# A fused decoder layer: the mixer's log decay spread by ScalarE in 16 copies, and the gate's projection, tanh and gating put ahead of the turning of y

## The chip, the cores and the metric

The kernel runs on one core of one Trainium2 chip. The metric is the device time of one execution in microseconds (us). Engines: PE (TensorE; PEld is its weight load), DVE (VectorE), ACT (ScalarE), POOL (GpSimd), SP (SyncE, which here issues DMAs only).

## The reference

One decoder layer over 32 sequences of 256 tokens of width 256: a mixer with a layer norm behind it, an attention over a context of 77 tokens, and a layer of 8 experts with 2 chosen per token. The change lies in the mixer alone:

```
zxBCdt = x @ in_proj_w.T                      # z, xc, Bm (8), Cm (64), dtm (64)
dt = softplus(Bm + dt_bias)
xh = silu(depthwise_causal_conv(xc, conv_w, conv_b)).reshape(B, L, 8, 64)
a_bar = exp(dt * -exp(A_log))
h = a_t[:, :, None, None] * h + b_t[:, None, None, :] * x_t[..., None]   # for every token t
y_t = einsum('bhdn,bn->bhd', h, c_t)
y = (y + xh * D_param) * silu(z)
x = layernorm(x + rms_norm(y, norm_w) @ out_proj_w.T)
```

## The kernel before, in words

The program is a chain of phases: mixer (`mixer_phase`), keys and values, attention, experts, finish. The mixer takes one sequence a turn. The recurrence is not run token by token. Within each half of 128 tokens (index c, `NT` = 2) it is a product with a weight matrix exp(sum of log decays) for each of the 8 heads. For that the log decay `l_dt` (128 tokens x 8 heads) is multiplied with the triangle `upto` into `lm` (128 x 8 x 128) for each half: this is **spread_l** (L732 to L739), one GpSimd product of 1024 columns a half. PE multiplies `lm` by the matrix `after` (**decay(c)**, L365 to L379), ACT takes the exponential (**exp_decay(c)**, L502 to L508), DVE weighs it with the scores (**weigh(c)**, L610 to L618), and PE forms y with it (**mix**, L393 to L405).

The work is a software pipeline written by hand. Each engine has a list of stages, each with a lag: in turn s the stage works on sequence s minus its lag. `run_steps` (L78 to L98) walks the list in order, with the first 4 and the last turns written out and the others in a loop of 2 sequences a round. There are 32 sequences and lags up to 2 on PE and ACT, so 34 steps there. An engine does its stages strictly in the order of its list, and waits on semaphores within each stage.

The order on PE (L435 to L437): in_x (the projection of xc), turn_y (y of two turns ago is turned into PSUM), in_z (the gate's projection), in_bc, step_size, scores, decay(0), turn_x, decay(1), out (the output projection), mix, mix_off.

The order on ACT (L533 to L535): take_xc, squares, y_high, tanh_z, take_bc, exp_decay(0), exp_rc, take_x, exp_decay(1), tanh_conv, softplus. The tables for tanh and exp and for ln alternate, so there are two table loads a turn, at tanh_z (L477) and at softplus (L531).

The order on DVE (L701 to L704): the high part of the next x, the first taps of the convolution, y_low, gate, bias_dt, mask_g, taps, weigh(0), weigh(1), taps, normalise, add_d, silu_conv, log_decay, residual.

The order on POOL (L787 to L788): x_low, inv_rms, scale_x, join (three products and sums that make y; L743 to L756), spread_l, inv_std. SP loads x two turns ahead and stores the result.

Two PSUM tiles bind stages together. `p23` holds the turned y (`ps_yT`) and also the two banks that decay(c) writes. y is split from it into a high part (y_high on ACT, L479 to L483) and a low part (y_low on DVE, L583 to L585), so decay(0) waits until y_low of the sequence before is done:

```
def y_low(b):
    dve.wait_ge(s_yhi, b.count(1, 1))
    dve.tensor_tensor(yT_lo[:, :, :], ps_yT, yT_hi[:, :, :].bitcast(F32), ALU.subtract).then_inc(s_ylo, 1)
```

`p45` holds the gate's projection, which tanh_z (L473 to L477) and gate (L575 to L581) read, and then the turned x.

Of the kernel before, what the change touches and what calls it, by code (L numbers as in the profile page):

```python
# [8 lines left out]
ALU = mybir.AluOpType  # L9
ACT = mybir.ActivationFunctionType  # L10
# [5 lines left out]
P = 128  # L16
# [3 lines left out]
NT = L // P  # L20
# [96 lines left out]
def mixer_phase(nc, n_seq, signals, following, xT, x, x1, w_in, w_out, norm_w, conv_w, conv_b, A_log, D_param, dt_bias, masks):  # L117
# [7 lines left out]
    H, N_STATE, D_CONV, DI = 8, 64, 4, 512  # L125
# [6 lines left out]
    with ExitStack() as ctx:  # L132
# [20 lines left out]
        upto, after, ident = mk[:, 0, :], mk[:, 1, :], mk[:, 2, :]  # L153
        spare = sb("spare", [P, 1])
# [21 lines left out]
        l_dt = sb("l_dt", [P, 2, NT * H])  # L176
        lm = sb("lm", [P, NT, H, P])
# [111 lines left out]
        def _(pe):  # L289
# [75 lines left out]
            def decay(c):  # L365
                def run(b):

                    if c == 0:
                        pe.wait_ge(s_lm, b.count(1, 1))
                        if not b.before(1):  # L370
                            pe.wait_ge(s_ylo, b.ago(1).count(1, 1))
                    else:
                        pe.wait_ge(s_exp, b.count(NT, 1))
                    for j in range(2):
                        last = pe.matmul(p23[:, j, :], after,
                                         lm[:, c, 4 * j:4 * j + 4, :].rearrange("p h t -> p (h t)"),
                                         start=True, stop=True)
                    last.then_inc(s_E, 1)
                return run  # L379
# [41 lines left out]
            def out(b):  # L421
# [11 lines left out]
                last.then_inc(s_out, 1)  # L433

            run_steps(pe, n_seq, [  # L435
                (in_x, 0), (turn_y, 2), (in_z, 0), (in_bc, 0), (step_size, 0), (scores, 1), (decay(0), 1), (turn_x, 1),
                (decay(1), 1), (out, 2), (mix, 1), (mix_off, 1)])  # L437

        @block.scalar
        def _(act):  # L440
            act.wait_ge(s_w_in, 16)
            for part in W_PARTS:
                act.activation(w_hi[:, :, part], w_stage[:, :, part], ACT.Copy).then_inc(s_whi_a, 1)
            act.wait_ge(s_load, 16 * N_LOADS)
            act.activation(a_neg[:, :], a_neg[:, :], ACT.Exp).then_inc(s_whi_a, 1)

            def take_xc(b):

                act.wait_ge(s_xc, b.count(1, 1))
                if b.before(1):  # L450
                    act.wait_ge(s_pow, 2)
                else:
                    act.wait_ge(s_conv, b.ago(1).count(12, 12))
                    act.wait_ge(s_sx, b.ago(1).count(1, 1))
                act.activation(xc_pad[:, :, D_CONV - 1:], ps_xc, ACT.Copy).then_inc(s_pad, 1)
                for m in range(MI):
                    last = act.activation(conv[:, m, :], ps_xc[:, m, :], ACT.Identity,  # L457
                                          bias=cb[:, m:m + 1], scale=cw[:, m, D_CONV - 1:D_CONV])
                last.then_inc(s_tap, 1)

            def squares(b):
                for c in range(NT):
                    act.wait_ge(s_y, b.count(NT, c + 1))
                    if c:
                        act.wait_ge(s_sq, b.count(NT, c))
                    elif not b.before(1):
                        act.wait_ge(s_sq, b.ago(1).count(NT, NT))
                    if not b.before(2) and c == 0:
                        act.wait_ge(s_ri, b.ago(2).count(2, 1))
                    act.activation(sq[:, :], y[:, b.par, c, :], ACT.Square, accum_out=ss[:, b.par, c:c + 1]  # L470
                                   ).then_inc(s_sq, 1)

            def tanh_z(b):  # L473
                act.wait_ge(s_z, b.count(1, 1))
                if not b.before(1):
                    act.wait_ge(s_zs, b.ago(1).count(1, 1))
                act.activation(z_t[:, :, :], p45[:, :, :], ACT.Tanh, scale=0.5).then_inc(s_zt, 1)  # L477

            def y_high(b):  # L479
                act.wait_ge(s_yT, b.count(1, 1))  # L480
                if not b.before(1):
                    act.wait_ge(s_out, b.ago(1).count(1, 1))
                act.activation(yT_hi[:, :, :], ps_yT, ACT.Copy).then_inc(s_yhi, 1)  # L483

            def take_bc(b):
                act.wait_ge(s_bc, b.count(1, 1))
                if not b.before(2):
                    act.wait_ge(s_g, b.ago(2).count(1, 1))
                for w in range(2):
                    last = act.activation(bc[:, b.par, w, :], ps_bc[N_STATE * w:N_STATE * w + N_STATE, :], ACT.Copy)  # L490
                last.then_inc(s_bcc, 1)

            def exp_rc(b):

                act.wait_ge(s_g, b.count(1, 1))
                act.wait_ge(s_gm, b.count(1, 1))
                if not b.before(1):
                    act.wait_ge(s_or, b.ago(1).count(1, 1))
                    act.wait_ge(s_cx, b.ago(1).count(1, 1))
                act.activation(rc[:, :], ps_rc, ACT.Exp).then_inc(s_rc, 1)  # L500

            def exp_decay(c):  # L502
                def run(b):
                    act.wait_ge(s_E, b.count(NT, c + 1))
                    if not b.before(1):
                        act.wait_ge(s_mt, b.ago(1).count(NT, c + 1))
                    act.activation(e_x[:, c, :, :].rearrange("p h t -> p (h t)"),
                                   p23[:, :, :].rearrange("p b t -> p (b t)"), ACT.Exp).then_inc(s_exp, 1)  # L508
                return run

            def take_x(b):
                act.wait_ge(s_T, b.count(1, 1))
                if not b.before(1):
                    act.wait_ge(s_Y, b.ago(1).count(NT, NT))
                    act.wait_ge(s_xd, b.ago(1).count(1, 1))
                    act.wait_ge(s_cx, b.ago(1).count(1, 1))
                act.activation(x_t[:, :, :], p45[:, :, :], ACT.Copy).then_inc(s_xt, 1)

            def tanh_conv(b):
                act.wait_ge(s_conv, b.count(12, 12))  # L520
                if not b.before(1):
                    act.wait_ge(s_sx, b.ago(1).count(1, 1))
                act.activation(conv_t[:, :, :], conv[:, :, :], ACT.Tanh, scale=0.5).then_inc(s_ct, 1)

            def softplus(b):
                act.wait_ge(s_na, b.count(1, 1))
                act.activation(v_ex[:, :], v_na[:, :], ACT.Exp).then_inc(s_dex, 1)
                act.wait_ge(s_dex, b.count(1, 1))
                if not b.before(1):
                    act.wait_ge(s_sp, b.ago(1).count(1, 1))  # L530
                act.activation(v_ln[:, :], v_ex[:, :], ACT.Ln, bias=1.0).then_inc(s_dln, 1)  # L531

            run_steps(act, n_seq, [  # L533
                (take_xc, 0), (squares, 2), (y_high, 2), (tanh_z, 0), (take_bc, 0), (exp_decay(0), 1), (exp_rc, 1),
                (take_x, 1), (exp_decay(1), 1), (tanh_conv, 0), (softplus, 0)])  # L535

        @block.vector
        def _(dve):
# [90 lines left out]
            def log_decay(b):  # L629
# [3 lines left out]
                                         op0=ALU.max, op1=ALU.add).then_inc(s_sp, 1)  # L633
                dve.wait_ge(s_sp, b.count(1, 1))
                if not b.before(2):
                    dve.wait_ge(s_lm, b.ago(2).count(1, 1))
                    dve.wait_ge(s_g, b.ago(2).count(1, 1))
                dve.tensor_tensor(l_dt[:, b.par, :].rearrange("p (c h) -> p c h", c=NT),
                                  v_sp[:, :].rearrange("p (c h) -> p c h", c=NT),
# [54 lines left out]
            def prep_once(b):  # L694
# [4 lines left out]
                    prep_out()  # L699

            run_steps(dve, n_seq, [  # L701
                (prep_once, 0), (x_high_next, 0), (taps(0, 1), 0), (y_low, 2), (gate, 0), (bias_dt, 0), (mask_g, 1),
                (taps(1, 2), 0), (weigh(0), 1), (weigh(1), 1), (taps(2, 3), 0), (normalise, 3), (add_d, 1),
                (silu_conv, 0), (log_decay, 0), (residual, 2)], spare=2)  # L704

# [1 line left out]
        def _(pool):  # L707
# [7 lines left out]
            def scale_x(b):  # L715
# [12 lines left out]
                                              x_t[:, c, :].rearrange("p (h d) -> p h d", h=H),  # L728
                                              d_b[:, :].unsqueeze(2).to_broadcast([P, H, HD]), ALU.mult)
                last.then_inc(s_xd, 1)  # L730

            def spread_l(b):  # L732

                pool.wait_ge(s_l, b.count(1, 1))
                if not b.before(1):
                    pool.wait_ge(s_E, b.ago(1).count(NT, NT))
                for c in range(NT):
                    last = pool.tensor_tensor(lm[:, c, :, :],
                                              l_dt[:, b.par, H * c:H * c + H].unsqueeze(2).to_broadcast([P, H, P]),  # L739
                                              upto.unsqueeze(1).to_broadcast([P, H, P]), ALU.mult)  # L740
                last.then_inc(s_lm, 1)

            def join(b):  # L743

# [38 lines left out]
            def x_low_next(b):  # L783
                if not (b.known() and b.value() + 1 >= n_seq):
                    x_low(b.ago(-1))

            run_steps(pool, n_seq, [  # L787
                (x_low_next, 0), (inv_rms, 2), (scale_x, 1), (join, 1), (spread_l, 0), (inv_std, 2)], spare=2)  # L788


class Unit:
# [1520 lines left out]
```

## Time and profile before

| | |
|---|---|
| median of 3 runs | 2477.99 us (2472.6 to 2484.72) |
| profiled execution | 2475.47 us, span in the profile 2473.7 us |
| busy over the whole span | PE 2201.1 us (89%), DVE 1793.5 (73%), ACT 1394.5 (56%), POOL 1243.3 (50%) |
| mean granted clock of PE | 0.944 |
| PE granted clock in 40 slices of the span | 9999999999997987999999999999988999999955 |
| DVE busy in the same slices, in tenths | 7888888888895312676776776776755777777778 |
| POOL busy in the same slices, in tenths | 3767677677664432032232232232244777766656 |

One slice is 62 us. The mixer fills the first 13 slices, some 790 us. The attention fills about slices 17 to 30. A busy share says how long an engine worked in a stretch, and not who waited for it; for that the views of waits and of the order in time are read.

### The profile page before, as it was taken

What the parts mean: (1) busy time and instruction counts of PE and PEld (TensorE: products, weight loads), DVE (VectorE), ACT (ScalarE), POOL (GpSimd) and SP (SyncE); (2) the same over time, 40 slices, a digit from 0 to 9 for tenths busy, and PEclk for the clock granted to TensorE, in tenths of its full rate; (3) what the DMA queues carried; (4) which work ended last, traced back from release to release, by engine and by line L of the source; (5) the groups of instructions that cost most, each with busy time, mean ns of one, the idle gap of its engine ahead of it and who ended that gap; (6) DMA issues with size and microseconds to landing.
All of it is one profiled execution on the core that took longest, in us unless ns stands there. A gap on an engine that the chain in (4) does not pass through costs nothing. (4 is left out here: it accounts for less than half of the span.)

```text
span 2473.7 us, 53288 instructions
## 1 busy us (share of the span) xinstructions
PE 2201.1 (89%) x15804; PEld 1917.0 (77%) x15805; DVE 1793.5 (73%) x4428; ACT 1394.5 (56%) x3046; POOL 1243.3 (50%) x1347
## 2 busy tenths in 40 slices
PE   7999999999995866999999999999968999999766
PEld 5777777777774755888888888888858999999733
DVE  7888888888895312676776776776755777777778
ACT  5556556565562321666666666666635666655433
POOL 3767677677664432032232232232244777766656
PEclk9999999999997987999999999999988999999955
DMA  4101111101001797233222212211136777776588
GB/s 143 31 26 38 34 30 38 34 30 38 30 29 51 259 327 237 82 107 110 63 63 64 64 62 63 66 61 62 59 113 221 233 254 237 246 233 221 164 282 269
DMA packets 169263, 295.27 MB, mean 119 GB/s; under 512 B 26204, under 2 KB 107620, under 8 KB 169188
## 3 DMA queue, kind: packets, MB, share of 16 engines
q1 hardware_dynamic: 155140, 257.62, 32.2%
q0 software_dynamic: 12960, 35.67, 4.0%
q10 hardware_dynamic: 1088, 1.07, 0.1%
q8 instruction: 37, 0.61, 0.1%
q14 instruction: 38, 0.31, 0.0%
HBM read 192.52 MB, written 101.77 MB: 119 GB/s over the span
## 5 line engine op out<-in xcount | busy, mean ns | idle before, releaser
L1460 ACT ACTIVATE b_wk_f<-b_ps_s,b_nmx 128x77 f32<-128x77 f32 x1024 | 233.7, 347 | 15.5 <-DVE b_nmx L1508 15.5
L570 DVE SCALAR_TENSOR_TENSOR a_conv<-a_xc_pad,a_cw,a_conv 128x256 f32<-128x256 f32 x384 | 236.6, 675 | 7.8 <-ACT a_conv L457 7.8
L1468 ACT ACTIVATE b_pT<-b_ps_pT 77x1024 f32<-77x1024 f32 x128 | 130.7, 1021 | 142.5 <-PE b_ps_pT L1366 142.5
L2056 POOL DMA_INDIRECT made_scratch<-c_o_s,c_to x142 | 151.0, 1064 | 90.9 <-issue 43.3
L112 PE MATMUL c_ps_h<-c_xT_hi,c_w 128*128 128x256 f32 x568 | 167.6, 295 | 26.0 <-DMA c_b_c<-in_c_b 18.7
L1524 DVE TENSOR_TENSOR b_oT_lo<-b_ps_oT,b_oT_hi 128x512 fp32r<-128x512 f32 x128 | 88.0, 688 | 134.9 <-ACT b_oT_hi L1474 133.2
L1928 ACT ACTIVATE c_hid<-c_ps_h,c_b_c 128x256 f32<-128x256 f32 x284 | 111.1, 474 | 104.9 <-issue 66.5
L112 PE MATMUL c_ps_o<-w,c_h_hi 128*128 x568 | 160.4, 282 | 6.6 <-DVE c_h_lo L1972 6.6
L1451 ACT ACTIVATE b_qT<-b_ps_q,b_bq_s 128x256 f32<-128x256 f32 x256 | 107.5, 472 | 100.3 <-PE b_ps_q L114 96.9
L113 PE MATMUL c_ps_h<-c_xT_lo,c_w 128*128 128x256 f32 x568 | 161.7, 285 | 0.0
L114 PE MATMUL c_ps_h<-c_xT_hi,c_w 128*128 128x256 f32 x568 | 161.5, 284 | 0.0
L1354 PE MATMUL b_ps_s<-b_kz,b_qT 128*128 128x154 f32 x1024 | 156.6, 295 | 4.9 <-ACT b_wk_f L1460 4.8
L114 PE MATMUL c_ps_o<-w,c_h_lo 128*128 x568 | 159.9, 282 | 0.0
L113 PE MATMUL c_ps_o<-w,c_h_hi 128*128 x568 | 159.8, 281 | 0.0
L112 PE MATMUL b_ps_q<-b_xT_hi,b_wq_hi 128*128 128x256 f32 x512 | 156.0, 305 | 2.4 <-DVE b_xT_lo L1500 1.5
L1972 DVE TENSOR_TENSOR c_h_lo<-c_hid,c_h_hi 128x1024 fp32r<-128x1024 f32 x71 | 94.8, 1335 | 86.3 <-ACT c_h_hi L1937 69.3
L112 PE MATMUL b_ps_out<-b_wo_hi,b_oT_hi 128*128 128x256 f32 x512 | 156.9, 306 | 0.0
L1718 POOL TENSOR_TENSOR b_e<-b_euler,b_gap 128x2 f32<-128x2 f32 x32 | 23.6, 736 | 256.6 <-DVE b_gap L1573 256.6
L1745 POOL DMA_INDIRECT sent_scratch<-b_x_t,b_pos x128 | 127.1, 993 | 46.3 <-issue 46.3
L114 PE MATMUL b_ps_q<-b_xT_hi,b_wq_lo 128*128 128x256 f32 x512 | 145.8, 285 | 0.0
L1354 PEld LDWEIGHTS b_ps_s<-b_kz,b_qT 128*128 128x128 f32 x1024 | 141.3, 190 | 5.6 <-issue 5.6
L113 PE MATMUL b_ps_q<-b_xT_lo,b_wq_hi 128*128 128x256 f32 x512 | 145.5, 284 | 0.0
(269 smaller groups left out, 7855.6 us busy)
## 6 DMA issues: line engine op xcount, KB each, us to landing
c_w<-parts_scratch SPq DMA_DIRECT2D x71, 1024.0 KB
c_xa<-sent_scratch SPq DMA_DIRECT2D x71, 260.0 KB
parts_scratch<-w SPq DMA_DIRECT2D x32, 512.0 KB, 3.3
d_got<-made_scratch SPq DMA_DIRECT2D x32, 512.0 KB, 5.2
keys_scratch<-k_k_s SPq DMA_DIRECT2D x8, 1232.0 KB, 6.1
b_kz<-keys_scratch SPq DMA_DIRECT2D x64, 154.0 KB, 2.8
b_vv<-values_scratch SPq DMA_DIRECT2D x32, 308.0 KB
a_xT_f<-in_xT SPq DMA_DIRECT2D x32, 256.0 KB, 3.0
```

The source lines that it names most:

```text
L112: eng.matmul(out, lh, rh, start=start, stop=False)
L113: eng.matmul(out, lh, rl, start=False, stop=False)
L114: return eng.matmul(out, ll, rh, start=False, stop=stop)
L570: dve.scalar_tensor_tensor(out=conv[:, m, :], in0=xc_pad[:, m, k:k + L], scalar=cw[:, m, k:k + 1], in1=conv[:, m, :], op0=ALU.mult, op1=AL ...
L1354: last = pe.matmul(s_scores[:, i, 2 * j:2 * j + 2, :], qT[:, u.par, i, P * j:P * j + P], kz[:, b.par, :, GM * g + i, :], start=True, stop= ...
L1451: last = act.activation(qT[:, u.par, i, :], ps_q[:, L * i:L * i + L], ACT.Identity, bias=bq_s[:, m:m + 1], scale=HD ** -0.5)
L1460: last = act.activation(pe_[:, u.par, c, :], s_scores[:, c // (C // GM), c % (C // GM), :], ACT.Exp, bias=nmx[:, u.par, c:c + 1])
L1468: act.activation(pT[:, u.par, :, :], ps_pT[0:LK, :, :], ACT.Copy).then_inc(s_pTc, 1)
L1745: pool.indirect_dma_start(routing.sent, bass.IndirectOffsetOnAxis(pos[:, b.par, 2 * c + n:2 * c + n + 1], 0), x2_t[:, b.par, c, :], None). ...
L1928: last = act.activation(hid[:, T * m:T * m + T], ps_h[t.par][:, m // 2, T * (m % 2):T * (m % 2) + T], ACT.Gelu, bias=b1_c[:, t.par, m:m + 1])
L1972: dve.tensor_tensor(h_lo[:, t.par, :], hid[:, :], h_hi[:, t.par, :].bitcast(F32), ALU.subtract).then_inc(s_hlo, 1)
L2056: pool.indirect_dma_start(routing.made, bass.IndirectOffsetOnAxis(to[:, t.slot, c:c + 1], 0), o_s[:, t.par, c, :], None).then_inc(s_sent[t ...
```

## The change

ScalarE takes over spread_l: for each half c it writes 8 copies of the triangle `upto`, each scaled by the log decay of one head (a scale per partition). There is one stage for each half, spread_l(0) after squares and spread_l(1) after y_high. PE's decay(c) waits for its half alone. On PE in_z comes ahead of turn_y; on ACT tanh_z comes ahead of y_high; on DVE gate comes ahead of y_low. GpSimd's list loses spread_l. log_decay, which writes `l_dt` again two sequences later, now waits for both halves.

```diff
@@ decay(c), on PE
+                    pe.wait_ge(s_lm, b.count(NT, c + 1))
                     if c == 0:
-                        pe.wait_ge(s_lm, b.count(1, 1))
                         if not b.before(1):
                             pe.wait_ge(s_ylo, b.ago(1).count(1, 1))
@@ PE's order
-                (in_x, 0), (turn_y, 2), (in_z, 0), (in_bc, 0), (step_size, 0), (scores, 1), (decay(0), 1), (turn_x, 1),
+                (in_x, 0), (in_z, 0), (turn_y, 2), (in_bc, 0), (step_size, 0), (scores, 1), (decay(0), 1), (turn_x, 1),
@@ ScalarE
+            def spread_l(c):
+                def run(b):
+
+                    act.wait_ge(s_l, b.count(1, 1))
+                    if not b.before(1):
+                        act.wait_ge(s_E, b.ago(1).count(NT, c + 1))
+                    for h in range(H):
+                        last = act.activation(lm[:, c, h, :], upto, ACT.Copy, scale=l_dt[:, b.par, H * c + h:H * c + h + 1])
+                    last.then_inc(s_lm, 1)
+                return run
@@ ScalarE's order
-                (take_xc, 0), (squares, 2), (y_high, 2), (tanh_z, 0), (take_bc, 0), (exp_decay(0), 1), (exp_rc, 1),
+                (take_xc, 0), (squares, 2), (spread_l(0), 1), (tanh_z, 0), (y_high, 2), (spread_l(1), 1), (take_bc, 0), (exp_decay(0), 1), (exp_rc, 1),
@@ log_decay, on DVE
-                    dve.wait_ge(s_lm, b.ago(2).count(1, 1))
+                    dve.wait_ge(s_lm, b.ago(2).count(NT, NT))
@@ DVE's order
-                (prep_once, 0), (x_high_next, 0), (taps(0, 1), 0), (y_low, 2), (gate, 0), (bias_dt, 0), (mask_g, 1),
+                (prep_once, 0), (x_high_next, 0), (taps(0, 1), 0), (gate, 0), (y_low, 2), (bias_dt, 0), (mask_g, 1),
@@ GpSimd
-            def spread_l(b):
-
-                pool.wait_ge(s_l, b.count(1, 1))
-                if not b.before(1):
-                    pool.wait_ge(s_E, b.ago(1).count(NT, NT))
-                for c in range(NT):
-                    last = pool.tensor_tensor(lm[:, c, :, :],
-                                              l_dt[:, b.par, H * c:H * c + H].unsqueeze(2).to_broadcast([P, H, P]),
-                                              upto.unsqueeze(1).to_broadcast([P, H, P]), ALU.mult)
-                last.then_inc(s_lm, 1)
@@ GpSimd's order
-                (x_low_next, 0), (inv_rms, 2), (scale_x, 1), (join, 1), (spread_l, 0), (inv_std, 2)], spare=2)
+                (x_low_next, 0), (inv_rms, 2), (scale_x, 1), (join, 1), (inv_std, 2)], spare=2)
```

## Rows read from the trace of the kernel before

**Rows 1.** Stretches: us, busy time of each engine, granted clock, DMA share, GB/s.
```profile
core 0: us, PE busy (x) PEld busy (x) DVE busy (x) ACT busy (x) POOL busy (x), PEclk, DMA share, GB/s
201.20:601.20 400.00, 369.03 (x2384) 306.91 (x2384) 354.76 (x615) 234.99 (x377) 276.55 (x222) 1.00 0.11 33
```

**Rows 2.** Waits from 200 to 600 us: us in total, times, longest.
```profile
PE a_p L418 <- POOL a_y L756: 26.6, 17, 1.6
...
PE a_p L375 <- ACT a_e_x L507: 4.4, 18, 0.2
```

**Rows 3.** Order in time, ACT, one turn: start, duration, instruction, idle before.
```profile
401.20 1.03 ACT L455 ACTIVATE a_xc_pad<-a_p 128x1024 f32<-128x1024 f32 x1 [2.72 <-PE a_p L114]
402.12 1.93 ACT L457 ACTIVATE a_conv<-a_p,a_cb,a_cw 128x256 f32<-128x256 f32 x4
403.91 0.65 ACT L470 ACTIVATE a_sq<-a_y 128x512 f32<-128x512 f32 x1
...
405.38 1.01 ACT L483 ACTIVATE a_yT_hi<-a_p 128x1024 fp32r<-128x1024 f32 x1
406.40 1.28 ACT L477 ACT_TABLE_LOAD   x1
407.69 1.02 ACT L477 ACTIVATE a_z_t<-a_p 128x1024 f32<-128x1024 f32 x1
408.62 0.76 ACT L490 ACTIVATE a_bc<-a_p 64x256 f32<-64x256 f32 x2
411.37 1.03 ACT L507 ACTIVATE a_e_x<-a_p 128x1024 f32<-128x1024 f32 x1 [2.00 <-PE a_p L375]
...
424.81 1.02 ACT L455 ACTIVATE a_xc_pad<-a_p 128x1024 f32<-128x1024 f32 x1 [2.89 <-PE a_p L114]
```

**Rows 4.** Order in time, PE, the same turn.
```profile
400.88 0.28 PE L114 MATMUL a_p<-a_xT_hi,a_w_lo 128*128 128x256 f32 x1
402.73 1.09 PE L418 MATMUL a_p<-a_mk,a_y 128*128 128x128 f32 x8 [1.57 <-POOL a_y L756]
403.57 0.48 PE L112 MATMUL a_p<-a_w_hi,a_xT_hi 128*128 128x512 f32 x1
...
406.46 0.28 PE L112 MATMUL a_p<-a_xT_hi,a_w_hi 128*128 128x256 f32 x1
...
409.37 1.96 PE L375 MATMUL a_p<-a_lm,a_mk 128*128 128x512 f32 x4
...
412.45 1.98 PE L375 MATMUL a_p<-a_lm,a_mk 128*128 128x512 f32 x4 [0.24 <-ACT a_e_x L507]
```

**Rows 5.** Order in time, DVE, the same turn.
```profile
404.73 3.30 DVE L570 SCALAR_TENSOR_TENSOR a_conv<-a_xc_pad,a_cw,a_conv 128x256 f32<-128x256 f32 x4
407.96 1.21 DVE L585 TENSOR_TENSOR a_yT_lo<-a_p,a_yT_hi 128x1024 fp32r<-128x1024 f32 x1
409.10 1.20 DVE L580 SCALAR_TENSOR_TENSOR a_zs<-a_z_t,a_p 128x1024 f32<-128x1024 f32 x1
...
411.04 1.66 DVE L570 SCALAR_TENSOR_TENSOR a_conv<-a_xc_pad,a_cw,a_conv 128x256 f32<-128x256 f32 x4
```

**Rows 6.** Order in time, POOL, the same turn.
```profile
402.63 3.94 POOL L738 TENSOR_TENSOR a_lm<-a_l_dt,a_mk 128x1024 f32<-128x1024 f32 x2
```

**Rows 7.** Order in time, ACT, in the attention: eight short activations in a row.
```profile
1001.84 1.82 ACT L1460 ACTIVATE b_wk_f<-b_ps_s,b_nmx 128x77 f32<-128x77 f32 x8
```

**Rows 8.** Stretches with pauses of PE and what follows them, columns as in rows 1.
```profile
828.00:832.00 4.00, 0.00 (x0) 0.00 (x0) 0.60 (x1) 0.00 (x0) 1.87 (x2) 0.78 0.79 316
832.20:835.00 2.80, 2.80 (x7) 1.98 (x8) 0.49 (x1) 0.00 (x0) 1.71 (x2) 0.50 0.99 339
...
32.30:35.00 2.70, 2.70 (x4) 1.15 (x4) 2.70 (x5) 1.41 (x3) 1.33 (x1) 0.50 0.00 0
```

**Rows 9.** Order in time, PE, the first turn with a decay.
```profile
32.28 3.78 PE L375 MATMUL a_p<-a_lm,a_mk 128*128 128x512 f32 x4 [2.42 <-POOL a_lm L738]
...
37.72 2.21 PE L375 MATMUL a_p<-a_lm,a_mk 128*128 128x512 f32 x4
```

## The prediction

> **What bounds the kernel now.** I read the stretch view first, then the waits, then the order of time on each engine through one turn of the mixer's loop. The change touches only the mixer, the first 790 us. In its steady part PE is busy 369 us of 400 at a granted clock of 1.00, DVE 355, POOL 277, ACT 235 [rows 1]. A turn takes 400/17 = 23.5 us, since 17 waits of each kind stand in 400 us [rows 2]. PE waits in two places only: 26.6/17 = 1.56 us a turn before the turning of y, for GpSimd's last product y, and 4.4/17 = 0.26 us at the second decay, for ScalarE's exp [rows 2]. So PE is the bound, with 1.8 us a turn to win, and ACT's 41% of idle time seems free to take GpSimd's work.
>
> The order of time says where that idle time lies. Call T the end of in_x on PE (401.16) and D the start of decay(0) (409.37) [rows 4]. From T to D a chain also runs over ACT: take_xc (401.20), squares (403.91), y_high (405.38 to 406.39), then the table load and tanh_z (407.69 to 408.71), take_bc (408.62) [rows 3]. ACT has no pause there. DVE's y_low ends at 407.96 + 1.21 = 409.17, 0.2 us before D, because the taps in front of it took 3.30 us [rows 5] while GpSimd spread the decay for 3.94 us [rows 6]. ACT's idle time is elsewhere: before exp (2.00 us at 411.37) and before the next take_xc (2.89 us at 424.81) [rows 3]. D waits for y_low because yT and the decay share the PSUM tile p23: decay(0) waits on s_ylo. So D - T = 8.2 us, and from D to the next T (424.77, when take_xc starts at 424.81 [rows 3]) 15.4 us, which are PE's own work but for 0.24 us [rows 4].
>
> **The parts, against this execution's 2475.5 us.** It is 2.5 us under the median of the three runs.
>
> 1. in_z moves ahead of turn_y on PE. y is ready at 402.7; PE, released at T, gets there only after in_z, 2.9 us (403.57 to 406.46) of the 5.8 us from 403.57 to 409.37 [rows 4], at 404.1. The 1.57 us wait goes. What is late next is below. PE is now ready for decay(0) after the turning (402.73 to 403.57, with its pipeline 1.0 us) and 5.8 us of in_z, in_bc, step_size and scores: T + 6.8 us. No DMA and no step of SP moves.
>
> 2. GpSimd loses 3.94 us a turn [rows 6]. Behind it stand inv_std, x_low and inv_rms, which nobody on the path waits for, so the loss itself brings nothing. The taps lose their company and may take 1.7 us in place of 3.3, but the gate in front of y_low will wait for ACT anyway: nothing.
>
> 3. ACT gets 2 x 8 copies of 128x128 with a scale per partition. No such row exists. Below it 128x77 took 1.82/8 = 0.228 us each [rows 7], above it 128x256 with scale and bias took 1.93/4 = 0.483 us each [rows 3]. A straight line between gives 0.30 us, so 8 copies 2.4 us, of which the last 0.1 overlaps what follows: I take 2.3 us, and keep 1.8 and 3.8 us as ends.
>
> The Trainium skill (ScalarE: Activation LUTs, What ACT_TABLE_LOAD costs) gives an ACTIVATE with one pointer operand as about 280 ns + 0.833 ns an element, with 93 ns of overlap back to back. By that 8 copies are about 2.35 us, an estimate that would put the sum 1.5 us higher.
>
> 4. The order on ACT. y_high used to follow squares; now spread_l(0) and tanh_z with its table load stand between. In the turn from T: take_xc and squares until T + 4.2 (405.38 - 401.16) [rows 3]; spread_l(0) 2.3, until 6.5; table load 1.29, until 7.8; tanh 1.0, until 8.8. DVE's gate follows for 1.2 us [rows 5] beside y_high (1.0 us), until 10.0. Then y_low, 1.2 us: 11.2, and the step to PE 0.05. So D = T + 11.3 in place of T + 8.2. PE, ready at T + 6.8, waits 4.5 us for y_low. The two waits removed and added are one row in the old profile (L418 for a_y) and another in the new (L375 for a_yT_lo). Net: +3.1 us a turn.
>
> 5. spread_l(1) and take_bc after y_high: from T + 9.7 over 2.3 and 0.76 us to 12.7. exp(0) can start only at D + 2.0 = 13.3 [rows 3, 4]: hidden. If copies cost 0.48 us each it would be late by about as much as D is moved again, so no more is added.
>
> 6. **The clock.** A PE pause of 4.5 us comes every turn. Today's 1.6 us never costs clock (1.00 over 400 us [rows 1]). Longer pauses do: in 828 to 832 PE stood still, the granted clock fell to 0.78 in that stretch and was 0.50 while PE worked again [rows 8]. The trace has ten pauses of over 3.4 us that began at full clock, those at the very start apart, and after all ten the row of the next work shows 0.50, the 1.2 GHz level. Even 2.42 us at 29.9 did it (0.50 in the stretch after it [rows 8]): decay(0) then took 3.78 us in place of 1.96, and decay(1) ended 7.65 us after D (37.72 + 2.21 - 32.28) [rows 9] in place of 5.06 (412.45 + 1.98 - 409.37) [rows 4]: +2.6 us. In the change the pause itself is longer and takes more of the slow stretch, so I take 2.2 us a turn. The ends are 0 and 2.6.
>
> The Trainium skill (TensorE: Matmul & The Clock Gate, HAM oscillation — how this bites in real kernels) tells of a loop in which every wait throttles PE again, so that each burst starts cold. By that rule it is every turn, as in my sum; the ten pauses agree.
>
> **Sum.** Both y_high(b-2) and tanh_z(b) exist in 30 of the 34 steps. 30 x (3.1 + 2.2) = 159 us. In the first turn ACT's copies delay exp(0) by about 2 us and in the last but one step y_high by 1 us: +3. 2475.5 + 162 = **2637 us**. The turn becomes 28.8 us.
>
> **Rivals.**
> - *The wait without the clock.* The pause is as in step 4, but the granted clock stays at 1.00, or falls in few turns only, because the pauses are spread or PE is busy enough around them. For it: no row shows a pause that returns every 27 us with PE busy in between, and the steady turn's 1.6 us leaves the clock alone. Against: all ten agree, and the shorter one at 29.9 too. 2475.5 + 30 x 3.1 + 3 = 2572 us. Chance 0.25.
> - *Faster: ACT's chain fits.* If y_low ended by T + 6.8, PE would never wait: 30 x 1.8 = 54 us less, 2421 us. It decides at D - T = 8.2: every tenth of a us below is 3 us won. This takes an ACT chain shorter by 3.1 us than my rows give; the copies are only 2.3 us of it, so even free copies leave 9.0 and a loss. Only a mistake about the order, for instance a table load that is placed elsewhere (1.29) together with cheap copies, gets there. Chance 0.06.
> - *The change does nothing.* GpSimd was not on the path and ACT takes it all in its idle time; the waits only change places. D - T stays near 8.2: 2475 us. Against: ACT has no pause between T and y_high. Chance 0.04.
> - *Copies at the upper end.* 3.8 us for eight: another 1.5 us a turn, 30 x 1.5 = 45 us, 2682 us. Chance 0.07.
>
> **How the numbers follow.** The forecast has 0.58. Its own range is 2595 (cheap copies, or the clock falls in half the turns) to 2675 (2.6 us for the clock, dearer copies). To hold 8 in 10 I go down to the second case with its copies at the low end: 30 x (2.6) + 3 = 81, near 2560; and up to 2675. Slower by over 0.5% (about what a measurement of this kernel can tell from no change): 0.58 + 0.25 + 0.07 = 0.90. Within 0.5%: 0.04. Faster: 0.06.
>
> **What would show it.** Right: waits of PE at L375 for y_low of some 4.5 us, some 30 times; none at L418 for y; no pause of ACT from take_xc to y_high; take_xc to take_xc 28 to 29 us; the granted clock of 200 to 600 us clearly under 1.00, about 0.9, with decay(0) near 3.8 us. Step 6 is wrong if that clock is 1.00; step 4 if PE's new wait is under 3 us; step 3 if the copies' pitch is far from 0.28 us. The forecast as a whole is wrong if the turn stays under 24 us.

## The result and the profile after

The changed kernel takes **2639.29 us** (median of 4 runs, 2634.48 to 2643.52), against 2475.3 us for the kernel before on the same chip. The ratio is 1.0667, with a 95% interval of 1.0611 to 1.0723: slower by 164 us. 2637 was forecast, with a range of 2560 to 2675.

The stretch of [rows 1] in the new profile, with the same columns:

```profile
core 0: us, PE busy (x) PEld busy (x) DVE busy (x) ACT busy (x) POOL busy (x), PEclk, DMA share, GB/s
200.00:600.00 400.00, 328.03 (x1926) 263.75 (x1924) 268.98 (x493) 255.84 (x528) 161.36 (x152) 0.85 0.09 26
```

PE is busy 328 us of 400, where it was 369 in [rows 1]. Its granted clock is 0.85 in place of 1.00. In the same 400 us GpSimd's load fell from 277 to 161 us and DVE's from 355 to 269, but there are fewer turns in them now. A turn (its length is in the table below) has 11.7 us of GpSimd's work where it had 16.2, and 19.5 us of DVE's where it had 20.8. Neither made the turn shorter. The waits of the same stretch (us in total, times, longest), to set beside [rows 2]:

```profile
PE a_p L375 <- DVE a_yT_lo L596: 71.1, 14, 5.2
DVE a_mt L627 <- ACT a_e_x L518: 67.2, 28, 2.7
...
DVE a_zs L591 <- ACT a_z_t L477: 48.2, 14, 3.5
```

The wait at L418 for y has gone from the list. In its place PE waits 71.1/14 = 5.1 us a turn before decay(0) for y_low. DVE in turn waits 48.2/14 = 3.4 us for tanh_z. One turn on ACT, in order of time:

```profile
400.66 1.03 ACT L455 ACTIVATE a_xc_pad<-a_p 128x1024 f32<-128x1024 f32 x1 [2.88 <-PE a_p L114]
401.58 1.92 ACT L457 ACTIVATE a_conv<-a_p,a_cb,a_cw 128x256 f32<-128x256 f32 x4
403.38 0.65 ACT L470 ACTIVATE a_sq<-a_y 128x512 f32<-128x512 f32 x1
...
404.84 2.43 ACT L509 ACTIVATE a_lm<-a_mk,a_l_dt 128x128 f32<-128x128 f32 x8
407.29 1.28 ACT L477 ACT_TABLE_LOAD   x1
408.58 1.02 ACT L477 ACTIVATE a_z_t<-a_p 128x1024 f32<-128x1024 f32 x1
409.50 1.02 ACT L483 ACTIVATE a_yT_hi<-a_p 128x1024 fp32r<-128x1024 f32 x1
410.41 2.44 ACT L509 ACTIVATE a_lm<-a_mk,a_l_dt 128x128 f32<-128x128 f32 x8
412.75 0.76 ACT L490 ACTIVATE a_bc<-a_p 64x256 f32<-64x256 f32 x2
416.04 1.02 ACT L518 ACTIVATE a_e_x<-a_p 128x1024 f32<-128x1024 f32 x1 [2.53 <-PE a_p L375]
```

ACT has no pause from take_xc to take_bc. y_high stands at 409.50, 8.9 us after T (400.62); it stood 4.2 us after T in [rows 3]. The same turn on DVE and then on PE:

```profile
403.54 2.71 DVE L581 SCALAR_TENSOR_TENSOR a_conv<-a_xc_pad,a_cw,a_conv 128x256 f32<-128x256 f32 x4
409.74 1.22 DVE L591 SCALAR_TENSOR_TENSOR a_zs<-a_z_t,a_p 128x1024 f32<-128x1024 f32 x1 [3.50 <-ACT a_z_t L477]
410.88 1.22 DVE L596 TENSOR_TENSOR a_yT_lo<-a_p,a_yT_hi 128x1024 fp32r<-128x1024 f32 x1
```

```profile
403.10 1.03 PE L418 MATMUL a_p<-a_mk,a_y 128*128 128x128 f32 x8
...
406.65 0.37 PE L363 MATMUL a_p<-a_l_dt,a_mk 128*128 128x8 f32 x2
412.25 3.75 PE L375 MATMUL a_p<-a_lm,a_mk 128*128 128x512 f32 x4 [5.22 <-DVE a_yT_lo L596]
415.79 1.91 PE L390 MATMUL a_p<-a_mk,a_sx 128*128 128x128 f32 x8
417.50 2.20 PE L375 MATMUL a_p<-a_lm,a_mk 128*128 128x512 f32 x4
```

PE is done with scores at 407.02 and waits until 412.25. decay(0) then takes 3.75 us, where it took 1.96 in [rows 4]. The stretches around that pause show the clock (columns as above):

```profile
400.60:407.00 6.40, 6.40 (x42) 5.58 (x40) 5.13 (x14) 6.25 (x17) 4.75 (x6) 1.00 0.14 41
407.10:412.10 5.00, 0.00 (x0) 0.00 (x0) 2.36 (x3) 4.97 (x10) 0.00 (x0) 0.58 0.00 0
412.30:417.30 5.00, 5.00 (x12) 2.83 (x13) 2.32 (x8) 2.29 (x6) 0.00 (x0) 0.50 0.00 0
417.40:424.00 6.60, 6.60 (x45) 5.47 (x44) 4.21 (x6) 2.05 (x2) 4.03 (x3) 0.94 0.00 0
```

The clock is at full before the pause, falls in it, and is 0.50, the 1.2 GHz level, for the first 5 us of work after it. It then rises again: 0.94 in the last row, and 1.00 in the row of 400.60 ahead of the pause.

The next table goes by the starts of take_xc and of decay(0) (D) over 26 turns in the middle of the mixer. T is put 0.04 us ahead of take_xc, as in the prediction (401.16 against 401.20). Means in us; the last column is the end of PE's last product of the mixer:

| kernel | turn | T to D | D to T | mixer ends at |
|---|---|---|---|---|
| before | 23.44 | 8.13 | 15.32 | 786.0 |
| changed | 29.02 | 11.57 | 17.44 | 957.0 |

So 3.4 to 3.5 of the 5.58 us a turn are the chain to y_low, and 2.1 are what follows D. The last products of the mixer, before and changed:

```profile
785.60 0.41 PE L114 MATMUL a_p<-a_wo_hi,a_yT_lo 128*128 128x256 f32 x1
```

```profile
956.61 0.41 PE L114 MATMUL a_p<-a_wo_hi,a_yT_lo 128*128 128x256 f32 x1
```

The mixer alone became 171 us longer. The phases behind it are the same in both programs, yet they took 1687.6 us in the profile before and 1675.7 us in this one. Over the profiles of all fourteen kernels they lie between 1676 and 1700 us. So a difference of whole times carries up to some 12 us either way that don't come from the mixer.

### The profile page after: what moved, and what is told of

The parts are those of the page before. It is cut to its first block and busy times, and to the rows that moved or that the text cites. A ratio compares the mean times of both kernels' runs of the same rounds, so it can differ in the third digit from the quotient of the medians.

```text
span 2632.7 us, 53799 instructions
## 1 busy us (share of the span) xinstructions
PE 2262.4 (86%) x15804; PEld 1946.1 (74%) x15805; DVE 1746.6 (66%) x4428; ACT 1548.7 (59%) x3558; POOL 1100.2 (42%) x1283
## 3 DMA queue, kind: packets, MB, share of 16 engines
q10 hardware_dynamic: 1088, 1.07, 0.1%
## 5 line engine op out<-in xcount | busy, mean ns | idle before, releaser
L375 PE MATMUL a_p<-a_lm,a_mk 128*128 128x512 f32 x256 | 186.6, 868 | 158.9 <-DVE a_yT_lo L596 152.9
L375 PEld LDWEIGHTS a_p<-a_lm,a_mk 128*128 128x128 f32 x256 | 63.1, 274 | 215.8 <-issue 212.4
L581 DVE SCALAR_TENSOR_TENSOR a_conv<-a_xc_pad,a_cw,a_conv 128x256 f32<-128x256 f32 x384 | 199.8, 580 | 13.9 <-ACT a_conv L457 13.2
L627 DVE TENSOR_TENSOR a_mt<-a_e_x,a_g_m 128x1024 f32<-128x1024 f32 x64 | 94.3, 1474 | 152.8 <-ACT a_e_x L518 152.8
L732 POOL TENSOR_TENSOR a_cx<-a_x_t,a_rc 128x512 f32<-128x512 f32 x32 | 33.4, 1045 | 378.1 <-ACT a_x_t L528 378.1
L112 PE MATMUL c_ps_h<-c_xT_hi,c_w 128*128 128x256 f32 x568 | 166.6, 293 | 24.7 <-DMA c_b_c<-in_c_b 20.0
L509 ACT ACTIVATE a_lm<-a_mk,a_l_dt 128x128 f32<-128x128 f32 x512 | 155.8, 391 | 0.0
```

The lines of the kernel that those rows point to most:

```text
L112: eng.matmul(out, lh, rh, start=start, stop=False)
L375: last = pe.matmul(p23[:, j, :], after, lm[:, c, 4 * j:4 * j + 4, :].rearrange("p h t -> p (h t)"), start=True, stop=True)
L509: last = act.activation(lm[:, c, h, :], upto, ACT.Copy, scale=l_dt[:, b.par, H * c + h:H * c + h + 1])
L581: dve.scalar_tensor_tensor(out=conv[:, m, :], in0=xc_pad[:, m, k:k + L], scalar=cw[:, m, k:k + 1], in1=conv[:, m, :], op0=ALU.mult, op1=AL ...
```

## The experiments

Twelve kernels ran. Ratios are to the kernel before on the same chip. Turn, its two parts and the end of the mixer are as defined above; the clock is that of 200 to 600 us.

| run | us | ratio, 95% interval | turn | T to D | D to T | clock | mixer ends at |
|---|---|---|---|---|---|---|---|
| a_filled | 2638.95 | 1.0661 [1.0622, 1.0700] | 28.74 | 11.58 | 17.17 | 0.91 | 952.7 |
| a2_filled_more | 2627.62 | 1.0615 [1.0563, 1.0667] | 28.08 | 12.10 | 15.98 | 0.94 | 938.7 |
| a3_filled_dense | 2597.50 | 1.0498 [1.0441, 1.0554] | 27.29 | 11.58 | 15.71 | 0.99 | 910.2 |
| f_one_copy | 2594.97 | 1.0503 [1.0468, 1.0537] | 27.35 | 10.27 | 17.07 | 0.88 | 902.3 |
| b_y_high_first | 2568.15 | 1.0369 [1.0331, 1.0406] | 26.44 | 8.96 | 17.48 | 0.91 | 880.8 |
| d_engine_only | 2577.84 | 1.0415 [1.0365, 1.0465] | 27.06 | 8.97 | 18.09 | 0.96 | 894.1 |
| c_orders_only | 2569.56 | 1.0390 [1.0347, 1.0433] | 26.51 | 9.31 | 17.20 | 0.90 | 876.0 |
| c2_orders_filled | 2529.43 | 1.0222 [1.0188, 1.0255] | 25.01 | 9.38 | 15.64 | 0.99 | 837.0 |
| h_pe_only | 2526.69 | 1.0195 [1.0144, 1.0246] | 24.95 | 8.10 | 16.85 | 0.91 | 828.2 |
| j_y_low_ahead | 2478.15 | 1.0003 [0.9974, 1.0032] | 23.71 | 6.63 | 17.08 | 0.96 | 790.8 |
| g_early | 2454.34 | 0.9934 [0.9909, 0.9959] | 22.85 | 6.59 | 16.26 | 0.98 | 769.6 |
| g2_step_size_ahead | 2437.73 | 0.9854 [0.9810, 0.9899] | 22.37 | 6.84 | 15.52 | 1.00 | 756.8 |

Within one run the clock doesn't fall in every turn, and each trace says in which turns it did. Of the 26 turns, those in which PE had the full clock from T to the next T have these means:

| run | turns at full clock | turn | D to T |
|---|---|---|---|
| before | 26 | 23.44 | 15.32 |
| a2_filled_more | 17 | 26.96 | 15.40 |
| a3_filled_dense | 20 | 26.96 | 15.39 |
| d_engine_only | 7 | 26.31 | 17.34 |
| c2_orders_filled | 21 | 24.63 | 15.32 |
| h_pe_only | 3 | 23.36 | 15.28 |
| j_y_low_ahead | 15 | 23.50 | 16.87 |
| g_early | 13 | 22.11 | 15.52 |
| g2_step_size_ahead | 26 | 22.37 | 15.52 |

The changed kernel, a_filled, f_one_copy, b_y_high_first and c_orders_only have no such turn.

**The price of the clock: the pause filled with work.** The theory (a later y_low, and a clock that falls in the pause) and its rival (the chain alone) differ in what happens if PE works through the pause, with y_low where it is.

```diff
# a_filled, on the changed kernel (a2_filled_more: range(8))
+                for _ in range(5):
                     pe.matmul(ps_g[:, 0:2, :].rearrange("p g t -> p (g t)"), bT[:, 0:P], cT, start=True, stop=True)
                     pe.matmul(ps_g[:, 2, :], bT[:, P:L], cT[:, P:L], start=True, stop=True)
# a3_filled_dense, on the changed kernel
-                for k in range(KD):
+                for k in list(range(KD)) * 7:
                     last = split3(pe, ps_bc, pair(w_hi, w_lo, slice(None), k, slice(C_BC, C_DT)),
```

> The changed kernel, in which PE forms the two products of scores five times in place of once in each turn, so that PE works through most of the pause before decay(0); D itself is not moved, since y_low sets it. Theory (pause of 5 us plus clock): the granted clock of the mixer goes back to 1.00, decay(0) to 1.96 us, D to T to 15.4 us, the turn from 29.0 to 27.0 us: 2639 - 60 = 2575 to 2585 us. Rival (the clock costs nothing, all of the loss is the chain over ScalarE): the same 2639 us, or a little more for PE's added work.

Measured 2638.95 us: a miss. The filler was too short. PE still waited 2.6 us, and decay(0) was still slow:

```profile
406.47 0.37 PE L364 MATMUL a_p<-a_l_dt,a_mk 128*128 128x8 f32 x2
409.44 3.64 PE L376 MATMUL a_p<-a_lm,a_mk 128*128 128x512 f32 x4 [2.60 <-DVE a_yT_lo L597]
```

So it said only that a pause of half the length costs nearly the same: D to T is 17.17 us, against 17.44.

> As the filled run before, with the two products of scores eight times in place of five: that run still left 2.2 to 2.5 us of pause and its granted clock was 0.91, with decay(0) at 3.6 us, so it had not tested the price of the clock. Seven repeats of 0.655 us are 4.6 us and leave some 0.4 us of pause. Theory: clock 1.00, T to D 11.6 us as before, D to T back from 17.4 to 15.4, turn 27.0: 2639 - 60 = 2580 us. Rival (the time from D to T is longer for another reason than the clock): again 2639 us, at a clock of 1.00.

Measured 2627.62 us, with a wide scatter (2605.8 to 2638.4). No PE pause over 0.7 us was left, but the clock still fell in 9 of the 26 turns (0.94). In 6 of these the filler itself ran at the 1.2 GHz level and pushed D back to T + 13.9. The 17 turns at full clock took 26.96 us, where 27.0 was expected, but the total missed both expectations.

> The changed kernel with the six products of in_bc done seven times in a row, some 4.3 us of dense work in the pause, in place of the scores; the run with scores eight times had no pause and yet 0.50 in every other turn, so the kind of filler may count. take_bc has time until T + 12. Theory: granted clock 1.00, T to D 11.6, D to T 15.4, turn 27.0 us, 2575 to 2585 us. Rival (more PE work costs as much as the clock gives): 2620 us or more.

Measured 2597.50 us, clock 0.99, T to D unchanged at 11.58, D to T 15.71. This one isolates the price: against the changed kernel the turn is 29.02 - 27.29 = 1.73 us shorter with D where it was, and the time 2639.3 - 2597.5 = 42 us. The expected 2575 to 2585 was missed by 12 us, because the clock still fell in 6 of the 26 turns. The stretches from D to the next T, in a turn at full clock and in the turn behind it, where it fell (columns as above):

```profile
258.90:274.20 15.30, 14.97 (x100) 12.27 (x101) 11.91 (x20) 6.98 (x13) 6.53 (x5) 1.00 0.11 34
285.90:302.70 16.80, 16.46 (x99) 12.86 (x100) 11.82 (x20) 6.96 (x13) 7.48 (x5) 0.91 0.10 31
```

At full clock D to T is 15.39 us, 0.07 us from the kernel before, and the turn 26.96 us. So the clock's whole price in the changed kernel is 29.02 - 26.96 = 2.06 us a turn, and nothing else of note is late between D and the next T.

**The price of the copies.** Each spread is one activation of 1024 columns with the first head's scale; the log decays of the other seven heads are left out.

```diff
-                    for h in range(H):
-                        last = act.activation(lm[:, c, h, :], upto, ACT.Copy, scale=l_dt[:, b.par, H * c + h:H * c + h + 1])
+                    last = act.activation(lm[:, c, :, :], upto.unsqueeze(1).to_broadcast([P, H, P]), ACT.Copy,
+                                          scale=l_dt[:, b.par, H * c:H * c + 1])
```

> The changed kernel, each spread_l(c) one activation of 1024 columns with the first head's scale in place of eight of 128 columns; the log decays of the other seven heads are left out. Theory: the spread takes 1.03 us in place of 2.43, D comes 1.4 us earlier, PE's pause is 3.7 us in place of 5.1 and still costs the clock: turn 27.6 us, 2639 - 42 = 2597 us. Rival (ScalarE's load as a whole counts, 2.8 us less a turn): 2639 - 84 = 2555 us.

Measured 2594.97 us, T to D 10.27: 1.3 us from the first spread alone. D to T is 17.07, 0.4 us less than in the changed kernel, with the clock at 0.88 in place of 0.85. This run can't say whether the second, shorter spread or the clock gave that. The filled runs can: with the second spread at full length and the full clock, D to T was 15.39 us, so it was hidden. The pause of 3.9 us still cost 1.8 us after D.

**The order against the engine.** Two halves of the change, each alone, and y_high put back.

```diff
# b_y_high_first, on the changed kernel (DVE: y_low ahead of gate again)
-                (take_xc, 0), (squares, 2), (spread_l(0), 1), (tanh_z, 0), (y_high, 2), (spread_l(1), 1), (take_bc, 0), ...
+                (take_xc, 0), (squares, 2), (spread_l(0), 1), (y_high, 2), (tanh_z, 0), (spread_l(1), 1), (take_bc, 0), ...
# d_engine_only: the same, and PE's order of before
-                (in_x, 0), (in_z, 0), (turn_y, 2), ...
+                (in_x, 0), (turn_y, 2), (in_z, 0), ...
# c_orders_only, on the kernel before (PE and DVE as in the changed kernel)
-                (take_xc, 0), (squares, 2), (y_high, 2), (tanh_z, 0), (take_bc, 0), ...
+                (take_xc, 0), (squares, 2), (tanh_z, 0), (y_high, 2), (take_bc, 0), ...
```

> The changed kernel with y_high ahead of tanh_z on ScalarE again, and y_low ahead of gate on DVE; PE keeps in_z ahead of turn_y, and ScalarE keeps the copies (spread_l(0), y_high, tanh_z, spread_l(1), take_bc). Theory: D at T + 8.9 us in place of T + 11.6, so PE's pause falls from 5.1 to 2.4 us; but exp(0) now stands behind tanh_z, spread_l(1) and take_bc until T + 13.1 and is 2.2 us late. The turn is 26.4 us with a full clock, up to 28.5 if the pauses still cost clock: 2560 to 2620 us. Rival (only y_high's place mattered, the second spread is free): turn 24.3 us, 2500 us.

Measured 2568.15 us, T to D 8.96 (8.9 expected): the place of y_high, with y_low ahead of the gate to match, is worth 2.6 us a turn. ACT's row of the turn shows the second spread and take_bc running up to exp(0) without a gap:

```profile
407.86 2.43 ACT L509 ACTIVATE a_lm<-a_mk,a_l_dt 128x128 f32<-128x128 f32 x8
410.20 0.76 ACT L490 ACTIVATE a_bc<-a_p 64x256 f32<-64x256 f32 x2
410.98 1.02 ACT L518 ACTIVATE a_e_x<-a_p 128x1024 f32<-128x1024 f32 x1
```

D was 407.03, so exp(0) began at D + 3.95. At full clock that would be 2 us late. Here decay(0) took 3.75 us at half clock and nearly all of the lateness is hidden behind it. D to T is 17.2 to 17.8 us in each turn, 1.9 to 2.5 over the kernel before: the two prices of some 2 us don't add.

> The kernel before with ScalarE's copies alone: the orders of PE and DVE are the old ones, on ScalarE spread_l(0) stands behind squares, then y_high, tanh_z, spread_l(1), take_bc. It differs from the run with y_high first only in PE's order: turn_y ahead of in_z. Theory: D at T + 8.9, exp(0) 2.2 us late, the same length of turn of 26.4 us, but PE's idle time comes in three short waits (1.6 before turn_y, 0.7 before decay(0), some 2 before decay(1)), so less clock is lost than there: 2560 us, at or under that run. Rival (PE's order saves its 1.6 us wherever it stands): 30 x 1.6 = 48 us slower than that run.

Measured 2577.84 us, clock 0.96, 10 us over the run above, and 13 us over it at the end of the mixer. D came at T + 8.97, as there. The clock was held better, but now exp(0) is late in earnest, as PE's own rows show:

```profile
414.27 1.96 PE L375 MATMUL a_p<-a_lm,a_mk 128*128 128x512 f32 x4 [0.61 <-DVE a_yT_lo L596]
416.61 1.06 PE L390 MATMUL a_p<-a_mk,a_sx 128*128 128x128 f32 x8 [0.38 <-DVE a_zs L591]
419.39 1.95 PE L375 MATMUL a_p<-a_lm,a_mk 128*128 128x512 f32 x4 [1.72 <-ACT a_e_x L518]
```

Its 7 turns at full clock have 17.34 us from D to T in place of 15.32: the 2 us are exp(0) alone. The theory had this run at or under the other; it came out slightly over, and the rival's 48 us are excluded. So ScalarE's copies, put behind squares and ahead of take_bc, cost 100 us (2577.84 against 2477.85 for the kernel before, measured beside it) even without the new orders.

> The kernel before with the three new orders alone; GpSimd spreads the log decay as before. Theory: ScalarE reaches the end of tanh_z at T + 6.5, gate and y_low follow until T + 8.9, PE is ready at T + 6.5 and pauses 2.4 us. Turn 24.3 us with a full clock: 2475 + 30 x 0.8 = 2500 us; with the clock lost in every turn 2560 us. Rival (GpSimd's spread in front of the taps is what holds PE, the orders bring the 1.8 us of waits): about 2430 us.

Measured 2569.56 us: the orders alone cost 92 us. T to D is 9.31 (8.9 expected; the taps, beside GpSimd's spread, end 0.3 us after tanh_z), and the clock falls in every turn. The rival of a gain is out.

```diff
# c2_orders_filled, on c_orders_only
+                for _ in range(5):
                     pe.matmul(ps_g[:, 0:2, :].rearrange("p g t -> p (g t)"), bT[:, 0:P], cT, start=True, stop=True)
                     pe.matmul(ps_g[:, 2, :], bT[:, P:L], cT[:, P:L], start=True, stop=True)
```

> The three orders alone on the kernel before, with the products of scores five times: four repeats of 0.655 us are 2.6 us and fill its pause of 2.7 us before decay(0). Theory: clock 1.00, T to D 9.3 us, D to T 15.4, turn 24.7 us: 2475 + 30 x 1.25 = 2513 us, 57 us under the 2570 without filling. Rival (clock without price): 2570 us.

Measured 2529.43 us, clock 0.99, T to D nearly unchanged at 9.38, D to T 15.64. The clock's price is 40 us here too. The rival is out; the expected 2513 was 16 us too low, in part because the clock still fell in 5 of the 26 turns. The others took 24.63 us, where 24.7 was expected.

**PE's order alone.**

```diff
# h_pe_only, on the kernel before
-                (in_x, 0), (turn_y, 2), (in_z, 0), (in_bc, 0), (step_size, 0), (scores, 1), ...
+                (in_x, 0), (in_z, 0), (turn_y, 2), (in_bc, 0), (step_size, 0), (scores, 1), ...
```

> The kernel before with PE's order alone: in_z ahead of turn_y. Theory: the 1.6 us wait before turn_y goes and comes back before decay(0), since y_low is still set by the taps beside GpSimd's spread: T to D 8.2, turn 23.5, within 0.5% of 2475 us. The pause of 1.6 us stands in another place; if the clock falls there now, up to 60 us more. Rival (PE gains its 1.6 us): 2430 us.

Measured 2526.69 us. The wait moves to decay(0) with its length kept (25.8/16 = 1.6 us), T to D is 8.10 as before, and yet 53 us are lost, 42 of them by the end of the mixer. The expectation had named this as the second case. Waits first, then the stretches around one pause:

```profile
PE a_p L375 <- DVE a_yT_lo L585: 25.8, 16, 1.6
```

```profile
400.10:402.20 2.10, 2.10 (x17) 1.90 (x15) 2.10 (x4) 2.08 (x4) 2.02 (x3) 1.00 0.00 0
402.30:403.80 1.50, 0.00 (x0) 0.00 (x0) 1.50 (x3) 1.48 (x4) 1.50 (x3) 1.00 0.00 0
403.90:407.00 3.10, 3.10 (x5) 1.21 (x6) 3.06 (x9) 0.20 (x1) 0.70 (x2) 0.58 0.00 0
```

The pause after step_size and scores is followed by 0.58 here, and the clock fell in 23 of the 26 turns. In the 3 others D to T is 15.28 us, as in the kernel before, so the loss is the clock's. The same pause after in_x was followed by 1.00 in every one of the old kernel's steady turns.

**A version that beats both.** ScalarE's copies move to where ScalarE was idle: behind tanh_conv, at the end of the turn, for the sequence whose decay is due one turn later. For that softplus and log_decay come earlier.

```diff
# g_early, on the changed kernel (DVE: y_low ahead of gate again)
-                (take_xc, 0), (squares, 2), (spread_l(0), 1), (tanh_z, 0), (y_high, 2), (spread_l(1), 1), (take_bc, 0), ...
-                (take_x, 1), (exp_decay(1), 1), (tanh_conv, 0), (softplus, 0)])
+                (take_xc, 0), (squares, 2), (y_high, 2), (tanh_z, 0), (take_bc, 0), ...
+                (take_x, 1), (exp_decay(1), 1), (softplus, 0), (tanh_conv, 0), (spread_l(0), 0), (spread_l(1), 0)])
# DVE
-                ... (taps(2, 3), 0), (normalise, 3), (add_d, 1), (silu_conv, 0), (log_decay, 0), (residual, 2)
+                ... (taps(2, 3), 0), (log_decay, 0), (normalise, 3), (add_d, 1), (silu_conv, 0), (residual, 2)
# g2_step_size_ahead, PE on top of that
-                (in_x, 0), (in_z, 0), (turn_y, 2), (in_bc, 0), (step_size, 0), (scores, 1), ...
+                (in_x, 0), (step_size, 0), (in_z, 0), (turn_y, 2), (in_bc, 0), (scores, 1), ...
```

> A version that may beat both: ScalarE's copies stand in its idle time at the end of the turn. ScalarE: take_xc, squares, y_high, tanh_z, take_bc, exp_decay(0), exp_rc, take_x, exp_decay(1), softplus, tanh_conv, spread_l(0), spread_l(1) of the same sequence; DVE: y_low ahead of gate again, log_decay behind the last taps; PE: in_z ahead of turn_y. The table load of tanh_z moves to tanh_conv. Theory: y_high ends at T + 5.2, DVE's taps without GpSimd beside them at T + 5.6, y_low at T + 6.8, D at T + 6.9 with no pause and full clock: turn 22.3 us, 2475 - 30 x 1.1 = 2440 us. Rival (log_decay waits for ln and holds back add_d and the product y, or the copies hold back take_xc): 2475 us or more.

Measured 2454.34 us, ratio 0.9934 [0.9909, 0.9959]. T to D is 6.59, 5 us below the changed kernel. D to T is 16.26 in place of 15.3, because the clock still fell in 13 of the 26 turns. The 13 others took 22.11 us, with 15.52 from D to T.

> The early version with step_size ahead of in_z on PE. In the early version D comes at T + 6.6 but the clock is 0.97 with no pause over 0.4 us, and D to T is 16.2 us; the small products of turn_y, step_size and scores stand in a row before decay(0). Theory: with step_size elsewhere the clock stays at 1.00, turn 22.3 us, 2440 us. Rival (the clock falls as often, y_low comes later): 2454 us or more.

Measured **2437.73 us**, ratio 0.9854 [0.9810, 0.9899]. The clock of 200 to 600 us is 1.00 and the turn 22.37 us, 1.07 under the kernel before; the mixer ends 29 us earlier. Its stretch, then ACT in order of time:

```profile
200.00:600.00 400.00, 386.94 (x2515) 323.12 (x2514) 329.08 (x646) 327.82 (x682) 223.88 (x198) 1.00 0.12 35
```

```profile
406.98 4.78 ACT L509 ACTIVATE a_lm<-a_mk,a_l_dt 128x128 f32<-128x128 f32 x16
411.67 1.00 ACT L455 ACTIVATE a_xc_pad<-a_p 128x1024 f32<-128x1024 f32 x1
412.57 1.91 ACT L457 ACTIVATE a_conv<-a_p,a_cb,a_cw 128x256 f32<-128x256 f32 x4
414.36 0.63 ACT L470 ACTIVATE a_sq<-a_y 128x512 f32<-128x512 f32 x1
...
416.08 1.03 ACT L483 ACTIVATE a_yT_hi<-a_p 128x1024 fp32r<-128x1024 f32 x1 [0.18 <-PE a_p L418]
417.01 1.01 ACT L477 ACTIVATE a_z_t<-a_p 128x1024 f32<-128x1024 f32 x1
```

The sixteen copies fill the time before take_xc, y_high follows squares, and the table load has left the stretch between them. PE is busy 387 us of 400.

```diff
# j_y_low_ahead, on h_pe_only: GpSimd keeps the spread
-                (prep_once, 0), (x_high_next, 0), (taps(0, 1), 0), (y_low, 2), (gate, 0), ...
+                (prep_once, 0), (x_high_next, 0), (y_low, 2), (taps(0, 1), 0), (gate, 0), ...
```

> GpSimd keeps the spread; PE has in_z ahead of turn_y, and DVE has y_low ahead of the first taps. Theory: y_low ends at T + 6.4, D at T + 6.6 in place of T + 8.1, gate at T + 9.3 holds turn_x back by some 0.9 us: turn 22.9 us, 2475 - 30 x 0.55 = 2458 us. Rival (DVE, with 21 us of work a turn, becomes the bound, or the clock falls): 2475 us or more.

Measured 2478.15 us, ratio 1.0003 [0.9974, 1.0032]. T to D is 6.63, as expected, but D to T grows to 17.08. The gate, now behind the taps, holds turn_x back: the 15 turns at full clock already have 16.87. The clock (0.96) adds the other 0.2 us.

```profile
PE a_p L390 <- DVE a_zs L580: 21.4, 17, 1.9
```

So an earlier D alone is given back. It paid only in the version that moved the spread off DVE's neighbour and into ScalarE's idle time.

## Why the prediction was right

The forecast of 2637 us stands beside a median of 2639.3. The path, the wait and the clock were as forecast; that the totals agree within 2 us is in part luck, as the sum below shows. By its steps:

- **Step 1 (in_z first) held.** The wait for y is gone. PE was ready at T + 6.4 (407.02 - 400.62), a little earlier than the 6.8 worked out. The run of this step alone shows that it had a cost that the step did not name: with no other change it moves the wait and loses 53 us (42 in the mixer), and its turns at full clock lose nothing.
- **Step 2 (GpSimd's loss brings nothing) held** in this order of stages. DVE's first taps took 2.71 us, not 1.7: three of the four took 0.47 to 0.48 us, and one took 1.51 and ended 0.28 us after GpSimd's x_low. They end 3.5 us before the gate.
- **Step 3 (copies)** was put at 2.3 us for eight and measured 2.43. The Trainium skill's rule (ScalarE: Activation LUTs, What ACT_TABLE_LOAD costs) gave an estimate of 2.35; the trace is 0.08 us above it.
- **Step 4 (the order on ACT) is the cause of most of the loss.** T + 11.3 was forecast for D and T + 11.57 measured; the pause of 4.5 us was 5.1. The 0.3 us more are the copies and two handoffs of 0.14 us (tanh_z to gate, y_low to PE). Putting y_high back, with y_low ahead of the gate, took 2.6 us off T to D; shortening the first spread took 1.3.
- **Step 5 (second spread hidden) held**: take_bc ended at 413.5, exp(0) started at 416.04. But the cover is mostly the slow clock's. At full clock decay(0) would end at 414.2, and the cover is 0.7 us. That is enough: the full-clock turns of the filled runs show no delay from D on.
- **Step 6 (the clock)** was put at 2.2 us a turn. D to T grew by 2.1, and the dense filler's turns at full clock gave 2.06 back. The bursts after the pauses start at half clock in every turn, as the Trainium skill describes it (TensorE: Matmul & The Clock Gate, HAM oscillation — how this bites in real kernels), and the trace agrees with 0.50 in 412.3 to 417.3. The step's evidence was thinner than it reads. The old trace has twelve pauses of over 3.4 us that began at full clock, not ten. Half clock follows all of them, but once (1829.83 to 1833.38) only 0.4 us after PE had begun again. And beside the pause of 2.42 us at 29.9, which cost the clock, stands one of the same length at 2293.1 which did not, nor did one of 2.22 us at 2191.6:

```profile
2293.20:2295.50 2.30, 0.00 (x0) 0.01 (x1) 1.73 (x6) 1.40 (x2) 1.81 (x2) 1.00 0.52 143
2295.60:2298.00 2.40, 2.40 (x21) 2.40 (x22) 2.28 (x10) 0.51 (x2) 1.53 (x3) 1.00 0.80 214
```

So for pauses as short as this the old trace said both.

The sum was nearer than its parts. The term of 30 turns x 5.3 us = 159 measured 5.58 us a turn, 8 us more in all, mostly from step 4; step 6 was 0.1 us long. The last T came at 894.1 in place of 729.4 us, 165 us later, and the mixer ended 171 us later where the sum had 162. The phases behind it then took 12 us less in this profile than in the one before, though the change doesn't touch them. That the forecast of the whole came out within 2 us of the median is luck of this size.

The rivals fell by their own conditions. The wait without the clock (2572 us) needed a granted clock of 1.00, and it was 0.85. "Faster" needed T to D under 8.2 us. It took another order to get there, and then the same copies on the same engine gained. "The change does nothing" needed D - T near 8.2 us, and it was 11.57. "Copies at the upper end" needed 3.8 us for eight, and they took 2.43.

What stays open: why the clock falls in some turns and not in others of the same kernel where PE has no pause over 0.7 us (9 of 26 turns with the small scores as filler, 13 of 26 in the early version). Moving step_size ended it in the early version; why was not tried. Why the untouched phases vary between 1676 and 1700 us is open too.

## What to carry to other kernels

An engine's idle share says nothing of when it is idle: here ScalarE was free 41% of the time, and not for one moment between in_x and decay(0). The same sixteen copies cost 100 us ahead of y_high and take_bc, where all that is queued behind them comes later. Put at the end of the turn, where ScalarE waited, and with their partners reordered, they belong to the version that is 36 us faster. When a change lengthens or moves a pause of PE, look at the granted clock on both sides of it before counting the pause alone. And where a change touches one phase, read the end of that phase as well as the total: here the rest of the program varied by 24 us by itself.

## What the runs showed of the hardware

A pause of 1.5 to 1.6 us was free after in_x (clock 1.00, turn 23.44 us) and cost 1.5 us a turn after turn_y, in_bc, step_size and scores (clock 0.91, turn 24.95). So in these two kernels what PE did ahead of the pause mattered for its price, and not its length alone. In the early version moving step_size away from decay(0) brought the clock from 0.98 to 1.00 and 17 us, with D 0.25 us later.

The 128x16 product at the head of log_decay (L632, 1.26 us in the kernel before, at L643 in the changed one) takes 0.17 us in the early version, where it stands behind the last taps. In the kernel before, with GpSimd's sum (L754) beside it, and in the early version:

```profile
399.10 2.20 POOL L754 TENSOR_TENSOR a_t<-a_t,a_off_r 128x512 f32<-128x512 f32 x1 [0.57 <-DVE a_off_r L680]
```

```profile
400.07 1.26 DVE L632 SCALAR_TENSOR_TENSOR a_v_sp<-a_v_dt,a_v_ln 128x16 f32<-128x16 f32 x1
```

```profile
414.19 0.17 DVE L643 SCALAR_TENSOR_TENSOR a_v_sp<-a_v_dt,a_v_ln 128x16 f32<-128x16 f32 x1
```

It has the same operands and shape. In the slow place it ends at 401.33, 0.03 us after the GpSimd sum (401.30). So it does in 31 of its 32 turns in each of the twelve traces where the two stand beside each other. The first taps show the like: in that turn of the kernel before one of the four took 2.11 us, the others 0.47, and it ended 0.27 us after GpSimd's spread. That these DVE instructions are held until the GpSimd one ends fits every turn, but no run takes the GpSimd sum away alone.
